# Cross-attention by query tiles with stationary probabilities and a chain per tile, in front of a routed MLP

## What is computed

```python
q = einsum(layernorm(x), Wq); k = einsum(ctx, Wk); v = einsum(ctx, Wv)   # per head of 8 numbers
energy = where(mask == 0, -1e20, einsum('nqhd,nkhd->nhqk', q, k))
attention = softmax(energy / sqrt(128), axis=3)
x = x + einsum('nhql,nlhd->nqhd', attention, v).reshape(N, 512, 128) @ Wo.T + bo
flat = layernorm(x); probs = softmax(flat @ router_w.T); topk_p, topk_i = top_k(probs, 2)
w = topk_p / topk_p.sum()
out = x + sum_e mlp_e(flat) * combine_e(w, topk_i) + mlp_shared(flat)
```

## Time and profile before

| | us |
|---|---|
| median of 3 runs | 163.5 |
| lowest, highest run | 161.9, 164.51 |
| the profiled execution | 163.0 |
| its span, first to last instruction | 161.3 |
| busy PE, DVE, ACT, POOL | 136.7, 93.0, 77.9, 93.0 |

### The profile page before, as it was taken

One profiled execution on the slowest core, in us unless ns is written; L12 is line 12 of the kernel. 1 busy time (PEld: TensorE's weight loads), 2 busy tenths in 40 slices (PEclk: granted clock), 3 DMA queues, 4 the chain that ended last, 5 costly groups with the idle time before them and its releaser, 6 DMA issues.

```text
span 161.3 us, 2858 instructions
## 1 busy us (share of the span) xinstructions
PE 136.7 (85%) x945; PEld 110.9 (69%) x945; DVE 93.0 (58%) x239; ACT 77.9 (48%) x178; POOL 93.0 (58%) x109
## 2 busy tenths in 40 slices
PE   6575869899999719988878599999999999999680
PEld 2344558667759406544357499999999999998270
DVE  1689999975966993460685554343333334361614
ACT  3299927944636514211530265555656565545500
POOL 4387927875953853007782277877876546566300
PEclk9999999999999975899999999999999999999999
DMA  5833994595000000001102978988867860020041
GB/s 122 263 140 130 256 256 135 149 285 199 13 4 0 0 0 0 0 0 36 50 21 60 298 255 296 269 256 242 275 190 229 249 206 26 10 89 19 4 131 65
DMA packets 14798, 21.08 MB, mean 131 GB/s; under 512 B 1820, under 2 KB 10402, under 8 KB 14784
## 3 DMA queue, kind: packets, MB, share of 16 engines
q1 hardware_dynamic: 12880, 18.35, 38.9%
q0 software_dynamic: 1472, 2.14, 3.9%
q10 hardware_dynamic: 432, 0.41, 0.8%
HBM read 16.20 MB, written 5.60 MB: 135 GB/s over the span
## 4 chain that ended last, share of the span: by engine, by line
PE 60%; DVE 14%; issue 8%; POOL 6%; DMA 5%; ACT 4%; DVEq 0%; POOLq 0%
PE ps L1056 17%; PE ps L1069 17%; PE ps L923 9%; POOL slots_dram L456 5%; PE ps L910 4%; DVE p_area L670 3%; DVE s_max L662 3%; PE ps L1026 2%; PE ps L1040 2%; PE ps L1016 2%; DMA small_sb<-small 2%; DMA g_area<-slots_dram 2%; DVE x_area L634 2%; PE ps L895 2%; PE ps L837 1%
## 5 line engine op out<-in xcount | busy, mean ns | idle before, releaser
L794 DVE TENSOR_TENSOR hid<-n_area 128x512 f32<-128x512 f32 x38 | 26.2, 693 | 36.4 <-ACT n_area L568 36.4
L466 POOL DMA_INDIRECT y_dram<-x_area,g_area x30 | 33.0, 1098 | 15.9 <-ACT x_area L584 11.3
L568 ACT ACTIVATE n_area<-ps 128x512 f32<-128x512 f32 x38 | 22.7, 598 | 20.1 <-PE ps L1056 16.0
L456 POOL DMA_INDIRECT slots_dram<-rows,slot x16 | 17.6, 1100 | 19.6 <-DVE slot L748 15.4
L387 POOL TENSOR_TENSOR n_area<-p_area,s_rec 128x616 f32<-128x616 f32 x16 | 19.5, 1222 | 15.5 <-DVE s_rec L683 15.1
L923 PE MATMUL ps<-p_area,v_area 128*128 128x512 f32 x40 | 20.5, 642 | 0.7 <-ACT p_area L515 0.7
L505 ACT ACTIVATE p_area<-p_area 128x616 f32<-128x616 f32 x16 | 11.5, 716 | 15.3 <-DVE p_area L670 15.3
L1056 PE MATMUL ps<-v_area,w 128*128 128x128 f32 x128 | 16.8, 276 | 0.7 <-ACT v_area L575 0.7
L1069 PE MATMUL ps<-w,hid 128*128 128x128 f32 x128 | 16.9, 275 | 0.0
L515 ACT ACTIVATE p_area<-ps 128x384 f32<-128x384 f32 (+1 forms) x32 | 12.1, 430 | 8.4 <-PE ps L910 8.3
L1056 PEld LDWEIGHTS ps<-v_area,w 128*128 128x128 f32 x128 | 15.5, 192 | 0.9 <-ACT v_area L575 0.9
(11 more groups left out here) (131 smaller groups left out, 220.9 us busy)
## 6 DMA issues: line engine op xcount, KB each, us to landing
p_area<-w_all SPq DMA_DIRECT2D x14, 512.0 KB, 4.6
w<-w_all SPq DMA_DIRECT2D x9, 512.0 KB, 4.2
slots_dram<-empty SPq DMA_DIRECT2D x2, 990.0 KB, 7.9
g_area<-slots_dram SPq DMA_DIRECT2D x6, 264.0 KB, 4.5
g_area<-y_dram SPq DMA_DIRECT2D x3, 256.0 KB, 3.9
x_area<-x SPq DMA_DIRECT2D x2, 256.0 KB, 3.2
y_dram<-x_area,g_area POOLq DMA_INDIRECT x30
...
```

The costliest lines, as they stand in the source:

```text
L456: pool.indirect_dma_start(out=slots_dram, out_offset=bass.IndirectOffsetOnAxis(ap=slot[:, b, k, t:t + 1], axis=0), in_=rows[:, b * TB + t, ...
L466: pool.indirect_dma_start(out=y_dram, out_offset=bass.IndirectOffsetOnAxis(ap=xg[:, i, ID:ID + 1].bitcast(U32), axis=0), in_=y_sb[:, i % Y ...
L568: act.activation(r[:, u % RSLOTS, :], ps[:, UP_BANK[u % UPBANKS], :], ACT.Relu).then_inc(relu_done, 1)
L794: dve.tensor_tensor(hid[:, u % HSLOTS, :], r[:, u % RSLOTS, :], r[:, u % RSLOTS, :], ALU.mult)\
```

## The change

- **Steps** go by tile first: k = 2q and 2q + 1 are the two halves of heads of tile q (q = 0 to 7). Before, a step's half changed every four steps.
- **Scores** are one fp32 matmul for each group of 4 heads, with the 32 rows (RG) of those heads as contraction; the two masks come first and then the two scores. Keys `kblk` are one DVE product per batch, straight from PSUM; the queries `xn_t` are one ACT copy. The splits, `spread_keys` and POOL's key blocks are gone; of the six `keep_warm` products between the first transposes one is left.
- **PV** has `prob_t` stationary (5 chunks of 128) and 72 columns moving: 64 of values and 8 of ones per head, which give the sums. DVE inverts the sums and multiplies the PV result (`attention_out`). exp writes straight into the buffer that PE transposes; DVE's sum and POOL's multiplication are gone.
- **Chain**: for each tile, PE transposes the attention result, projects it, DVE adds the residual and does the statistics (`residual`), POOL normalises and writes both copies of the row, PE transposes that and makes the logits, DVE takes the top (`top_of`). Tile q goes through it in steps 2q + 5 and 2q + 6 (QLAG = 5), the last two behind the loop. `route(0)`, `ranks(0)`, `weigh(0)` and `assign(0)` stand in steps 13 to 15; before they stood behind the loop.
- **POOL** sends the rows of batch 0 in pieces of 2, 2 and 4 between the last normalisations. The part from the first expert tile on is the same.

```diff
-TLAG = 3
+QLAG = 5
+VH = UH * HD
+VS = VH + UH
+VT_AT = 1
+RG = P // JH
...
-SENT_FIRST = 5
+SENT_FIRST = (2, 4)
...
+            def normalise(q):
+
+                pool.wait_ge(var2_ready, q + 1)
+                link(pool.tensor_tensor(rstd[:, 1, q:q + 1], var_eps[:, 1, q:q + 1], minus_half[:, 0:1], ALU.pow))
+                pool.tensor_scalar(rows[:, q, :, 0:D], x2[:, q, :].unsqueeze(1).broadcast_to([P, TOPK, D]),
+                                   mv[:, 1, q, 0:1], rstd[:, 1, q:q + 1], ALU.subtract, ALU.mult)\
+                    .then_inc(xn2_done, 1)
+
...
-            root_inverse(1, 0, 1)
-
-            def normalise(k):
-                pool.wait_ge(rec_done, k + 1)
-                at_least(pool, pt_done, 2 * (k - PNR + 1))
-                pool.tensor_tensor(prob_n[:, k % PNR, :, 0:SK], prob[:, k % 2, :, :],
-                                   s_rec[:, k % 2, :].unsqueeze(2).broadcast_to([P, UH, SK]),
...
             v_blocks(0)
-            for k in range(NU):
-                if k == 14:
-                    root_inverse(2, 1, 0)
-                normalise(k)
-                if k == 4:
-                    mask_to_bias(TB, NT)
-                if k in (3, 8):
-                    key_blocks(pool, kblk_lo, kq_lo, 1, k // 8)
-                if k == 0:
-                    v_blocks(1)
-                if k == 6:
+            v_blocks(1)
+            for b in range(B):
+                pool.tensor_copy(v_ones[:, b * CH:(b + 1) * CH, :, VH:VS],
+                                 head_rows[:, :, :].unsqueeze(2).broadcast_to([P, CH, 2, UH])).then_inc(vones_ready, 1)
+            root_inverse(1, 0, 1)
+            mask_to_bias(TB, NT)
+            add_bias(0)
+            add_bias(1)
+            for q in range(TB):
+                normalise(q)
+                if q == 0:
                     tables()
-                if k == 9:
-                    add_bias(0)
-                if k == 12:
-                    add_bias(1)
+            normalise(TB)
+            normalise(TB + 1)
 
             def send_rows(b, first, last):
 
                 pool.wait_ge(slots_set[b], 16)
                 pool.wait_ge(weight_done, b + 1)
-                pool.wait_ge(copy_done, b + 1)
                 pool.wait_ge(slot_done, b + 1)
...
-            send_rows(0, 0, SENT_FIRST)
-            root_inverse(3, 1, 1)
-            send_rows(0, SENT_FIRST, TOPK * TB)
+            send_rows(0, 0, SENT_FIRST[0])
+            normalise(TB + 2)
+            send_rows(0, SENT_FIRST[0], SENT_FIRST[1])
+            normalise(TB + 3)
+            send_rows(0, SENT_FIRST[1], TOPK * TB)
...
-            act.wait_ge(kq_done, 1)
-            act.activation(kq_hi[:, :, :], ps[:, PROB_BANK[1], 0:B * SK].rearrange("p (b k) -> p b k", k=SK),
-                           ACT.Copy).then_inc(kq_split, 1)
...
+                act.activation(xn_t[:, 0, t * P:(t + 1) * P], ps[:, X_BANK[t], 0:P], ACT.Copy).then_inc(xn_read, 1)
...
+                act.wait_ge(pt_done, k + 1)
+                at_least(act, pv_done, k - 1)
+                act.activation(prob_t[:, k % 2, :, :].rearrange("p c q -> p (c q)"),
+                               ps[:, PROB_BANK:PROB_BANK + 2, :].rearrange("p i s -> p (i s)")[:, 0:CH * P],
+                               ACT.Copy).then_inc(pt_read, 1)
+
...
+            def read_attn(q):
+                act.wait_ge(at_done, q + 1)
+                act.activation(attn_t[:, :], ps[:, MISC_BANK, 0:P], ACT.Copy).then_inc(at_read, 1)
+
+            def read_xn2(q):
+                act.wait_ge(xt2_done, q + 1)
+                act.activation(xn2_t[:, q // TB, q % TB * P:(q % TB + 1) * P], ps[:, MISC_BANK, 0:P], ACT.Copy)\
+                    .then_inc(xn2_read, 1)
 
...
+            def key_blocks(b):
+                dve.wait_ge(kq_done, 1)
+                dve.wait_ge(hmask_ready, 1)
+                dve.tensor_tensor(kblk[:, b, :, :],
+                                  ps[:, KQ_BANK, b * SK:(b + 1) * SK].unsqueeze(1).broadcast_to([P, JH, SK]),
+                                  group_mask[:, :].unsqueeze(2).broadcast_to([P, JH, SK]), ALU.mult)\
+                    .then_inc(kblk_ready, 1)
+
+            key_blocks(0)
             layer_norm_apply(0, 0, x_sb, xn, 0)
...
-            def probs_sum(k):
-                dve.wait_ge(exp_done, k + 1)
-                dve.tensor_reduce(s_sum[:, k % 2, :], prob[:, k % 2, :, :], AX_X, ALU.add).then_inc(sum_done, 1)
-
-            def probs_rec(k):
-                dve.wait_ge(sum_done, k + 1)
-                at_least(dve, norm_done, k - 1)
-                dve.reciprocal(s_rec[:, k % 2, :], s_sum[:, k % 2, :]).then_inc(rec_done, 1)
...
+            def attention_out(q):
+
+                dve.wait_ge(pv_done, 2 * q + 2)
+                pv = ps[:, PV_BANK, 0:2 * VS].rearrange("p (i v) -> p i v", v=VS)
+                dve.reciprocal(sum_rec[:, :, :], pv[:, :, VH:VS]).then_inc(rec_done, 1)
+                at_least(dve, at_done, q)
+                dve.wait_ge(rec_done, q + 1)
+                dve.tensor_tensor(attn[:, :].rearrange("p (i h d) -> p i h d", i=2, d=HD),
+                                  pv[:, :, 0:VH].rearrange("p i (h d) -> p i h d", d=HD),
+                                  sum_rec[:, :, :].unsqueeze(3).broadcast_to([P, 2, UH, HD]), ALU.mult)\
+                    .then_inc(attn_done, 1)
+
+            def residual(q):
+                dve.wait_ge(proj_done, q + 1)
+                dve.wait_ge(xbo_ready, q // TB + 1)
+                dve.tensor_tensor(x2[:, q, :], ps[:, MISC_BANK, 0:D], x_bo[:, q, :], ALU.add).then_inc(x2_done, 1)
+                dve.wait_ge(x2_done, q + 1)
+                link(dve.bn_stats(stats[:, 1, q, :], x2[:, q, :]))
+                link(dve.bn_aggr(mv[:, 1, q, :], stats[:, 1, q, :]))
+                dve.tensor_scalar(var_eps[:, 1, q:q + 1], mv[:, 1, q, 1:2], EPS, None, ALU.add).then_inc(var2_ready, 1)
+
+            def top_of(q):
+
+                b, t = q // TB, q % TB
+                dve.wait_ge(logit_done, q + 1)
+                link(dve.max(top[:, b, t, :], ps[:, MISC_BANK, 0:NE]))
+                dve.max_index(top_at[:, b, t, :], top[:, b, t, :], ps[:, MISC_BANK, 0:NE]).then_inc(top_read, 1)
...
-            for k in range(NU + 1):
-                if k == 0:
+            for k in range(NU):
+                q = (k - QLAG) // 2
+                if k == TB * 2 + QLAG + 2:
+                    dve.wait_ge(rank_done, 1)
+                if k >= QLAG and k % 2 == 1:
+                    if q > 0:
+                        top_of(q - 1)
+                    if q == TB + 1:
+                        read_ranks(0)
+                    attention_out(q)
+                scores_max(k)
+                if k == TB * 2 + QLAG + 2:
+                    weigh(0)
+                    assign(0)
+                if k >= QLAG and k % 2 == 1:
+                    residual(q)
+                scores_sub(k)
+                if k == 1:
                     dve.wait_ge(x_in[1], 16)
                     layer_norm_stats(0, x_sb, 1)
-                if k < NU:
-                    scores_max(k)
-                if k > 0:
-                    probs_sum(k - 1)
-                if k < NU:
-                    scores_sub(k)
-                if k > 0:
-                    probs_rec(k - 1)
-                if k == 2:
+                if k == 3:
                     layer_norm_apply(1, 0, x_sb, xn, 1)
...
-                if k == 14:
-                    residual(0)
-                    layer_norm_stats(1, x2, 0)
-                if k == 15:
-                    layer_norm_apply(2, 1, x2, xn2, 0)
-            route(0)
-            weigh(0)
-            assign(0)
+                if k == TB * 2 + QLAG:
+                    route(0)
             nets(0)
-            residual(1)
-            layer_norm_stats(1, x2, 1)
+            for q in (NT - 2, NT - 1):
+                top_of(q - 1)
+                attention_out(q)
+                residual(q)
...
-            def three(out_ap, w_h, w_l, m, m_l, start, stop):
...
                 for i in range(2):
-                    g = 2 * half + i
-                    dst = heads_of(2 * (k % 2) + i)
-                    q = slice(qt * P, (qt + 1) * P)
-                    pe.matmul(dst, lhsT=ident_bf[:, :],
+                    pe.matmul(heads_of(2 * (k % 2) + i), lhsT=ident_bf[:, :],
                               rhs=mask_bias[:, b * TB + qt, :].unsqueeze(1).broadcast_to([P, JH, SK]),
                               start=True, stop=False)
-                    heads = slice(g * JH, (g + 1) * JH)
-                    last = three(dst, xn_hi[:, b, q], xn_lo[:, b, q],
-                                 kblk_hi[:, b, heads, :], kblk_lo[:, b, heads, :], False, True)
+                q = slice(qt * P, (qt + 1) * P)
+                for i in range(2):
+                    dims = slice((2 * half + i) * RG, (2 * half + i + 1) * RG)
+                    last = pe.matmul(heads_of(2 * (k % 2) + i), lhsT=xn_t[dims, b, q], rhs=kblk[dims, b, :, :],
```

(71 more changed lines are left out.)

401 lines of the change are left out of this document (166 added, 235 removed).

## The result

The changed kernel took **173.3 us** in the median of four runs (172.0 to 175.18); the kernel before took 163.1 in the same session (161.9 to 164.51). The ratio is **1.062, 95% interval 1.048 to 1.077**: slower. Forecast was 159.2, in a range of 153 to 167. The changed kernel's profiled execution took 172.4 with a span of 170.6 and a mean clock of 0.883 (before 0.978).

A forecast was written before the change was run, and what follows sets the result against it. PE was taken to bound the loop (6.6 us a tile against a chain of 6.3). First expert transpose at 86.1 plus an unchanged 71.4 gave a span of 157.5; with 1.7 around it, 159.2 us, range 153 to 167.

The forecast's parts named there:

- The stretch behind T: T is the start of the first expert-tile transpose; from there to the span's end was forecast unchanged at 71.4 us.
- V(0) = 24.9: V(q) is when tile q's var_eps is done; the start-up through tile 0 was summed to 24.9 us.
- V(4) to V(5): Tile 5's stretch, with weigh and assign on DVE ahead of its residual: forecast 9.6 us, attention_out ending after 4.9.
- PV with ten 72-column instructions: PE's probability-times-value work per step, priced at 0.114 us an instruction, 1.1 us in all.
- The pow of one column: First half of POOL's normalise, on 128x1: taken as 0.6 us, midway between 0.2 and 1.04.
- tensor_scalar 0.8: Second half of POOL's normalise, 128x256: 0.8 us, making POOL's part 1.6 with handovers and a tile's chain 6.3.
- rival 1: POOL's normalise is slow, chain 7.0 us in the loop: +4.4, 163.6 in all; 0.22 shared with the drain rival.
- The score price: Four 32-row fp32 score instructions per PE step: 1.03 us, bounds 0.51 to 1.35, within a PE tile of 6.6.
- the rule cited in the prediction: The Trainium skill says changing tiling mode drains TensorE; each of two changes a step was priced at 0.16 us.
- Clock: ... two tiles lose about 1 each: After a 3.6 us PE wait for tile 5, half clock costs the last two tiles 2 us, V(7) 73.5 to 75.5.
- T = V(7) + 1.6 + 3 x 1.26 + 5.24: Last tile's normalise, its remaining scatters, then last scatter to first expert transpose: forecast 86.1 us.
- Rival 3: The clock falls inside the loop and stays: a tile 13.2 us of PE, +26 in the loop, 185 in all; chance 0.07.

The follow-up runs named there:

- g1: The kernel before, unchanged, run again for its trace on another chip: 162.0 us, beside a median of 163.4 for the kernel before.
- g4: Changed kernel with normalise's product on DVE, batch 0's scatters sent earlier, weigh and assign behind the last sub, no zero products: 161.8 us (before 163.4).
- h1: g2 with 12 more zero products around the transposes of batch 1's x at 18 to 20 us: 154.5 us, ratio to the kernel before 0.949.
- e3: Changed kernel with 8 unread zero products on PE at the start, before the first transpose of x: 172.0 us (before 169.8 on that chip).
- f3: e1 with the 128x256 product of normalise moved from POOL to DVE: 167.4 us (before 170.3 on that chip).
- h2: Changed kernel, nothing moved, with unread zero products in every PE wait where its clock fell: 165.1 us, ratio to the kernel before 1.015.
- e1: Changed kernel with 22 unread zero products in PE's wait ahead of tile 5's normalised rows: 171.6 us (before 169.8 on that chip).
- g2: g4's three moves on the changed kernel, plus zero products in PE's waits at the start, around tile 5 and in the tail: 163.3 us (before 163.4).
- f2: e1 with batch 0's scatters split 3, 5 and 0, none behind the last tile: 167.5 us, ratio to the kernel before 0.983.

## Why the prediction was wrong

**Right.** The stretch behind T: 71.4 or 71.5 in g1 to g4 and h1, wherever the clock stayed up. The front at full clock: first mask at 8.3 and V(0) = 24.9 (e3), the latter with luck, since six steps of scores cost 1.3 less than in the sum and its waits must have taken about as much more. V(4) to V(5): 9.5 for 9.6, also in part by luck: `attention_out` ended 5.1 behind V(4) instead of 4.9, what follows up to the slots took 3.4 instead of 3.75. PV with ten 72-column instructions: 1.08 for 1.1. The pow of one column: 0.56 to 0.58 for 0.6 (0.94 beside the squares). The four scatters left behind tile 7, which I named as what remains of the early slots.

**The term "tensor_scalar 0.8".** It measured 1.23 and POOL's part 2.0 instead of 1.6. I halved the rate of the nearest row for a conversion that turned out to be no part of the price: 1.11, the straight reading of the earlier trace rows, was 10% off. My terms also add up to 6.2 and not to the 6.3 written there. With 0.45 more on POOL and 0.3 more in handovers the chain was 6.97, and rival 1, "chain 7.0 in the loop", is what the loop did: +1.4 in four tiles. Undoing this one piece (f3) gave 6.38.

**The score price.** 1.03 was too high: 0.72, overlap, below my bound of 0.77 for three in series, as the four run in two pairs. PE's tile is 6.38 (f3, g4, h1), not 6.6. So I had chain and bound the wrong way round, and the surplus of 0.3 was useless as long as the chain was longer. Of drains, as the rule cited in the prediction has them, little can be there: the first score starts 0.23 behind the second mask, 0.09 more than that mask's 0.14, and the transposes start 0.35 behind the second pair of scores, no later than pair follows pair (0.36). I had 0.16 for each of two changes.

**The step "Clock: ... two tiles lose about 1 each".** This is the largest miss. The wait and its length were right (3.57 for 3.6), the price of a PV at half clock nearly so (two from 72.29 to 76.46, 2.1 each for 2.2). Wrong was the duration: I let the clock come back within two tiles, since before it was 0.58 in 61:66.5 and back behind it. Here it stayed at 0.50 until about 86. V(5) to V(7) took 20.15, and 13.8 where it was held (h2, e1): 6.3 for the clock instead of 2. (The 13.8 is itself 1.2 above the 12.6 of the sum, by the chain of 6.9 for a tile.) Two more falls weren't in the sum at all, at the start (2.3) and behind T (2.8 against 71.4).

**The step "T = V(7) + 1.6 + 3 x 1.26 + 5.24".** 10.6 measured 11.7, and 12.8 at full clock: pow 0.94 and product 1.23 or 2.29, both beside DVE's squares. I had taken POOL's prices from rows with DVE on other work.

**The account.** Span 170.6 against 157.5 is +13.1: V(0) +2.3, loop +1.4, V(5) -0.1, V(5) to V(7) +5.5, T +1.1, behind T +2.8, together 13.0. With the clock held, 7.9 us go away (h2, 170.6 - 162.7), and h2 still pays 0.9 at V(0) for the products in front of it and 1.5 behind T: the clock cost some 10 us, of which the forecast had 2. So some 8 us of the miss are clock, some 5 are chain and POOL. Rival 3 (clock) was the right kind of case in the wrong place: I asked whether the clock falls in the loop, where it held in this kernel, and priced it below one in ten; it fell on either side of it. It isn't impossible there: in g2 it was down until 40.6 (V(0) to V(1) took 11.5), and the 209 us of f3 may be of that kind.

**Why early slots didn't help.** Before, the sum of slots, eight scatters and gather set T. After, slots are known at 63.6, 8 us earlier, but the last of batch 0's rows leave POOL behind tile 7's normalise at 91.15. The order of POOL's list, not the slots, was the new wait; sending none of the eight behind tile 7 (f2) took off 2.6.
